# Head attention: one value job moved from step 15 to step 24, and the ring of score tiles counted through all batches

## The reference

```
x = x + L0_xattn(layernorm(x), ctx, ids, pointers)   # window of 3 context rows for each token
x = x + L0_ffn(layernorm(x))                         # 8 experts, top 2, and a shared one
x = x + L1_xattn(layernorm(x), ctx, ctx)             # 16 heads of width 8 over 1601 context rows
x = x + L1_ffn(layernorm(x))                         # 8 heads, 16 experts, top 2
```

```
qh, kh, vh = split_heads(q @ Wq + bq), split_heads(k @ Wk + bk), split_heads(v @ Wv + bv)
scores = einsum('bhsd,bhtd->bhst', qh, kh) / sqrt(8)
out = softmax(scores) @ vh ;  return merge_heads(out) @ Wo + bo
```

## Time and profile before

| what | us |
| --- | --- |
| median of 3 runs (1922.25 to 1926.83) | 1922.9 |
| time of the profiled execution | 1942.84 |
| its span, first to last instruction | 1940.5 |
| head attention, first to last exponential | 671 to 1491 |
| PE busy / DVE busy / ACT busy / POOL busy | 1731.0 / 1040.0 / 1349.4 / 241.4 |
| granted clock of TensorE, mean | 0.979 |

### The profile page before, as it was taken

One profiled execution on the slowest core, in us unless ns is written; L12 is line 12 of the kernel. 1 busy time (PEld: TensorE's weight loads), 2 busy tenths in 40 slices (PEclk: granted clock), 3 DMA queues, 4 the chain that ended last, 5 costly groups with the idle time before them and its releaser, 6 DMA issues.

```text
span 1940.5 us, 47109 instructions
## 1 busy us (share of the span) xinstructions
PE 1731.0 (89%) x19832; PEld 1118.3 (58%) x19832; DVE 1040.0 (54%) x2670; ACT 1349.4 (70%) x1589; POOL 241.4 (12%) x160
## 2 busy tenths in 40 slices
PE   0546999999999989999999999999988899999998
PEld 0335999999998844444444455445444455555554
DVE  3996222222224355555555555555456877777773
ACT  0334444444443489999999999999998667766765
POOL 6346000000000110000000000000000212111222
PEclk9777999999999999999999999999999999999999
DMA  8001000000000233333333333333250000000000
GB/s 284 1 1 47 1 1 1 1 1 1 1 1 1 63 81 84 81 83 82 81 80 81 76 80 71 80 75 79 62 128 4 1 6 6 7 1 6 6 6 11
DMA packets 36213, 85.68 MB, mean 44 GB/s; under 512 B 10649, under 2 KB 23330, under 8 KB 35618
## 3 DMA queue, kind: packets, MB, share of 16 engines
q1 hardware_dynamic: 33954, 76.30, 16.6%
q0 software_dynamic: 2048, 6.36, 1.1%
HBM read 30.43 MB, written 2.10 MB: 17 GB/s over the span
## 4 chain that ended last, share of the span: by engine, by line
PE 50%; ACT 20%; issue 12%; DVE 9%; DVEq 1%; ACTq 0%; POOL 0%; POOLq 0%
ACT C_probs L1909 18%; PE C_ps_s L692 14%; PE C_ps_s L679 10%; PE C_ps_s L1149 6%; PE C_ps_s L1158 6%; DVE C_den_t L2073 3%; PE C_ps_o L1806 3%; PE C_ps_o L1174 2%; PE C_ps_s L1791 2%; PE C_ps_p L1139 2%; DVEq L2036 1%; DVE D_gated L1377 1%; PE C_ps_p L1740 1%; PE C_ps_s L697 1%; PE C_ps_p L1747 1%
## 5 line engine op out<-in xcount | busy, mean ns | idle before, releaser
L1909 ACT ACTIVATE C_probs<-C_ps_s 128x1024 f32<-128x1024 f32 x832 | 774.0, 1062 | 47.4 <-PE C_ps_s L1791 47.0
L1806 PE MATMUL C_ps_o<-C_probs,C_values 128*16 128x256 f32 x6656 | 440.1, 382 | 6.4 <-DVE C_o_t L2069 5.7
L1237 ACT ACTIVATE D_hidden<-C_ps_s,D_b_up 128x1024 f32<-128x1024 f32 x256 | 275.4, 1114 | 135.6 <-PE C_ps_s L1149 135.3
L753 ACT ACTIVATE B_hidden<-C_ps_s,B_b_up 128x512 f32<-128x512 f32 x288 | 192.0, 689 | 197.0 <-PE C_ps_s L679 196.4
L692 PE MATMUL C_ps_s<-B_w_down,B_hidden 128*128 128x128 f32 x2304 | 277.5, 277 | 0.0
L692 PEld LDWEIGHTS C_ps_s<-B_w_down,B_hidden 128*128 128x128 f32 x2304 | 271.4, 193 | 10.4 <-ACT B_hidden L753 1.2
L1791 PE MATMUL C_ps_s<-C_queries,C_keys 32*128 32x256 f32 x3328 | 211.3, 328 | 39.0 <-ACT C_probs L1909 37.7
L1806 PEld LDWEIGHTS C_ps_o<-C_probs,C_values 128*16 128x16 f32 x6656 | 154.3, 95 | 145.0 <-ACT C_probs L1909 8.6
L1791 PEld LDWEIGHTS C_ps_s<-C_queries,C_keys 32*128 32x128 f32 x3328 | 126.6, 183 | 168.2 <-ACT C_probs L1909 121.5
L856 DVE SCALAR_TENSOR_TENSOR B_acc<-C_ps_s,B_gate,B_acc 128x128 f32<-128x128 f32 x224 | 63.1, 344 | 273.5 <-PE C_ps_s L692 273.5
L1149 PE MATMUL C_ps_s<-D_up_in,D_w_up_r 128*128 128x512 f32 x512 | 186.6, 446 | 1.8 <-ACT D_hidden L1237 1.8
(11 more groups left out here) (275 smaller groups left out, 1951.4 us busy)
## 6 DMA issues: line engine op xcount, KB each, us to landing
C_keys<-C_k_hi SPq DMA_DIRECT2D x128, 200.1 KB, 4.2
C_ctx_t<-ctx_t_dram SPq DMA_DIRECT2D x16, 800.5 KB, 4.4
C_keys<-C_k_lo SPq DMA_DIRECT2D x64, 200.1 KB, 4.1
C_queries<-C_q_hi SPq DMA_DIRECT2D x128, 32.0 KB, 2.3
B_w_up<-L_ffn_w_up_dram SPq DMA_DIRECT2D x1, 2304.0 KB
B_w_down<-L_ffn_w_down_dram SPq DMA_DIRECT2D x1, 2304.0 KB
C_queries<-C_q_lo SPq DMA_DIRECT2D x64, 32.0 KB, 2.3
C_queries<-C_blank SPq DMA_DIRECT2D x16, 128.0 KB, 2.6
```

The lines of the kernel that those rows point to most:

```text
L753: nc.scalar.activation(hidden[:, e % HB, c, :], ps_h[c][:], ACT.Gelu, bias=b_up[:, u:u + 1]).then_inc(s_hid, 1)
L1237: nc.scalar.activation(hidden[:, u % RING, :, :], ps_u[u % 2][:], ACT.Gelu, bias=b_up[:, u % PAIRS:u % PAIRS + 1]).then_inc(s_hid, 1)
L1806: m = T.matmul(ps_o[32 * j:32 * j + 2 * DK, g % 2, :], values[:, parity, kt, g * HG + j, :], probs[:, slot(parity, 2 * step + j // 2), j % ...
L1909: nc.scalar.activation(probs[:, slot(parity, n)], ps_s[bank(parity, n)][:], ACT.Exp, scale=SCORE_SCALE1).then_inc(s_exp, 1)
```

## The change

The value job with index 13 moves from step 15 to step 20, and the four value jobs that stood at steps 20 to 23 stand at steps 21 to 24. `FIN_AFTER`, the number of jobs that piece 0 of `finish` waits for, is counted from `JOB_AT` and goes from 14 to 13. Since no job stands at step 15 any more, PE waits for the branch's `s_top_read` ahead of piece 0 at step 16 as well. The score tile of a unit is now counted over all units of all batches, and `scores` always waits for the unit three places before, in step 0 too.

```diff
-        JOB_AT = {u: n for n, u in enumerate((*range(8), 9, 10, 11, 12, 13, 15, *range(20, 24)))}
+        JOB_AT = {u: n for n, u in enumerate((*range(8), 9, 10, 11, 12, 13, *range(20, 25)))}
...
-        def bank(parity, n):
-            return (n + parity * (UNITS % SRING)) % SRING
-
-        def bank_before(parity, n):
-            at = n - 1
-            while (bank(parity, at) if at >= 0 else bank(1 - parity, UNITS + at)) != bank(parity, n):
-                at -= 1
-            return at
+        def bank(k, n):
+            return (UNITS * k + n) % SRING
...
-                    before = max(bank_before(parity, 2 * step + i) for i in range(2))
-                    wait(pe, s_exp, UNITS * k + before + 1)
+                    wait(pe, s_exp, UNITS * k + 2 * step + 2 - SRING)
...
-                            m = T.matmul(ps_s[bank(parity, 2 * step + j // 2)][:, j % 2, i, :],
+                            m = T.matmul(ps_s[bank(k, 2 * step + j // 2)][:, j % 2, i, :],
...
                             if last:
                                 pe.wait_ge(experts.s_job_done, experts.before_choice)
+                            elif n == min(FIN_AT):
+                                pe.wait_ge(s_top_read, TOP_READS * (k + 2) + 1)
                             finish(k - 1, 1 - parity, jobs_to(k + 1) + (0 if last else FIN_AFTER), FIN_AT[n])
```

More of the change, by code:

```diff
@@ L1634, in head_attention @@
         done = ForExperts(
-            home=home, ps_p=ps_p, ps_o=ps_o, ps_u=[ps_s[bank(1, UNITS - 3)], ps_s[bank(1, UNITS - 2)]],
-            ps_e=ps_s[bank(1, UNITS - 1)], s_exp=s_exp, exps=UNITS * BATCH, s_fin_read=s_fin_read, fins=BATCH)
+            home=home, ps_p=ps_p, ps_o=ps_o, ps_u=[ps_s[bank(BATCH - 1, UNITS - 3)], ps_s[bank(BATCH - 1, UNITS - 2)]],
+            ps_e=ps_s[bank(BATCH - 1, UNITS - 1)], s_exp=s_exp, exps=UNITS * BATCH, s_fin_read=s_fin_read, fins=BATCH)
         experts = head_experts(ctx, nc, io, x_sb, ident, norm_after, done)
@@ L1908, in exps @@
                             act.wait_ge(dense.s_down, dense.downs - 2 + n // 2)
-                        nc.scalar.activation(probs[:, slot(parity, n)], ps_s[bank(parity, n)][:], ACT.Exp,
+                        nc.scalar.activation(probs[:, slot(parity, n)], ps_s[bank(k, n)][:], ACT.Exp,
                                              scale=SCORE_SCALE1).then_inc(s_exp, 1)
```

## The result

The kernel after takes 1905.04 us (median, 1900.41 to 1907.5), the kernel before on the same chip 1922.58; the ratio is 0.9893 [0.9878, 0.9908]. The prediction said 1905.7. The medians are 17.5 apart; the ratio stands for 20.6 less, its interval for 17.7 to 23.5. So an agreement to a few tenths of a microsecond is in part luck.

A forecast was written before the change was run, and what follows sets the result against it. ACT's back-to-back exponentials were taken to pace head attention, so only the pauses between them cost time. 11.3 - 0.5 + 0.9 + 5.5 = 17.2 us off the median 1922.9 gave 1905.7; own range 1902 to 1909, full range 1899 to 1914.

The forecast's parts named there:

- Part 1: Job leaves step 15, batches 1 to 13: pauses at units 32 and 34 go, smaller one at 36; gain 11.3 us.
- 13 x 1.2: Sign in the table of waits: PE's piece 1 of finish waits for POOL's multiply, some 13 x 1.2 us in all.
- Part 2: A job arrives at step 24: costs nothing in ordinary batches, covered by step 25; batches 0 and 14 differ.
- Batch 0: Pause ahead of unit 32 goes whole, but step 23's fuller job waits 0.24 more for DVE: +0.9 us.
- Batch 14: Statistics on DVE delay emptying step 23's job, so unit 50 comes 1.4 late, against a 0.87 gain: -0.5 us.
- Part 3: Seven odd-to-even batch borders: scores(0) waits for unit 50 only, the 0.68 pause and 0.10 overlap go; gain 5.5 us.
- (a): POOL's multiply lets PE go later than its span ends, gain at unit 36 vanishes: 4.5 us left, 1918.4; chance 0.08.
- (b): Batch borders gain nothing because scores(0) of even batches waits for a landing: gain 11.7, 1911.2 us; chance 0.06.
- (c): All idle time at units 32 and 34 goes, without piece 1 waiting for POOL: gain 32.2, 1890.7 us; chance 0.03.
- (d): Placing chain ends later than step 0 in 15 batches; slower once a further 1.1 us late each; chance 0.03.

The follow-up runs named there:

- the run with the job alone: Kernel before with its own choice of score tiles, but value jobs moved to the new steps and the new wait ahead of piece 0: 1910.38 us, ratio 0.9933.
- the run with the ring alone: Kernel after with the value jobs where they stood before, so score tiles are counted through all batches: 1919.07 us, 0.9977 of the kernel before.
- three products on POOL: Three unused 128 x 128 products ahead of POOL's second multiply half: 1939.84 us added to the kernel after, 1932.64 us added to the kernel before.
- one product: Kernel after with one unused 128 x 128 product ahead of the second half of POOL's multiply: 1912.59 us, ratio 0.9941.

## Why the prediction was right

**Part 1, 11.3.** Right in place and mechanism: scores(16) and (17) in time, piece 1 waits for POOL, unit 36 at 2.44 behind POOL's start. The size was a little low. The 13 pauses of batches 1 to 13 sum to 11.0, mean 0.85, with overlap 12.3; the same batches had 24.9 at units 32 and 34, so 12.6 went. The place of the excess of 1.3 is the branch. The last inversion of DVE in batch 3 of the kernel after, to be read beside the earlier trace rows:

```profile
839.95 1.75 DVE L2068 RECIPROCAL C_den_t<-C_den_t 128x256 f32<-128x256 f32 x1 [1.70 <-DVEq L2056]
```

DVE's idle time ahead of this inversion sums to 25.0 over batches 1 to 13 before and to 23.3 after, 1.65 less. It differs from execution to execution: over batches 1 to 14 it is 25.2 to 27.5 in the seven profiled executions of kernels without a job at step 15, and 27.4 to 29.4 in the three with one. So the excess may be chance; that the change shortens the branch a little isn't ruled out. And the pause ahead of unit 36 follows it batch by batch: it is this idle time less 0.93 to 0.96 in batches 1 to 13 (1.70 and 0.76 here). Because of the shorter branch the wait of PE for POOL came to 10.2 in all and not to 13 x 1.2, too; besides, the table of waits counts from the end of a record (1.06 for weigh) and the prediction from 0.87, which is 0.19 in each batch. The small pauses ahead of unit 30 in batches 6, 7 and 9 are missing as well (about 1.1 with overlap). I don't count that to the change: the run with the job alone (0.35 and 0.26) and the two runs with more work on POOL in the kernel after have such pauses in the same order of work on PE, so they differ between executions.

**Part 2.** Step 24 costs nothing in any batch, right. Batch 0: 1.07 and 0.59 became 0.82, with the overlap 0.9 as predicted. Batch 14: the pause ahead of unit 50 is there, 1.10 where 1.2 was expected, ended as described, by DVE's late emptying; PE waits 1.20 for it at 1397.11. The batch comes out at +0.1 instead of -0.5, since its pause ahead of unit 36 is only 0.87: DVE's idle time at the branch was 2.42 in this batch before and 1.89 after.

**Part 3, 5.5.** All seven pauses at the borders are gone, and no wait of step 0 names a transfer. The run with the ring alone gives 4.6, with 5.5 inside its interval.

**The sum.** 12.6 + 1.1 + 0.9 + 0.1 + 5.5 = 20.2 in the pair of profiled executions, less 1.2 at the start of batch 0 (pauses of 3.68 and 0.45 for 2.20 and 0.69, the clock at 0.79 from 662 to 670), is 19.0 against the 18.95 measured; predicted were 17.2, the medians say 17.5 and the ratio 20.6. Taking the saving of one execution off the median held because the 19.9 between them lay ahead of the stage.

**The rivals.** (a) falls: in all fourteen batches POOL is named as the releaser of piece 1, and in each of them PE starts 0.05 or 0.06 behind the end of its recorded span. The Trainium skill (Perfetto Trace Analysis, section GPSIMD Engine Instruction) calls that span unreliable; for this tensor_tensor the trace disagrees. (b) falls by the ring alone. (c), all idle time gone at 1890.7, needed piece 1 not to wait for POOL. With `finish` a step later it doesn't, and that kernel takes 1894.4; with the statistics moved as well, which (c) didn't count on, it is 1891. The price of the rival was about right and its condition was missing. (d), a late placing chain, shows nowhere, even in kernels another 14 us faster.

## What to carry to other kernels

Idle time of the bottleneck is worth what is left after the next-latest event has been put in its place: find that event by the same sum of start, duration and hand-over before counting the pause as gain, and what it takes is also what the next change can win. Where a fixed chain ends in the middle of a written-out order, look at moving its consumer one slot as well as the work around it: here that brought 7 to 11 us on top of the job's 13. And a wait added to an engine that is itself nearly saturated has to be priced with the chance that its clock falls afterwards.

## What was not expected of the hardware

**A short wait of PE can be followed by a stretch at the lower clock.** In the run with the ring alone, batch 13, PE idles 0.60 ahead of weigh and 1.24 behind the branch, and the next runs of matmuls take 1.6 to 1.7 times as long as usual (timeline of PE):

```profile
1345.28 1.08 PE L1741 MATMUL C_ps_p<-C_wv,C_ctx_t 128*32 128x128 f32 x16 [1.24 <-DVEq L2054]
1346.29 0.80 PE L1784 MATMUL C_ps_s<-C_queries,C_keys 32*128 32x256 f32 x8
1347.02 1.82 PE L1799 MATMUL C_ps_o<-C_probs,C_values 128*16 128x256 f32 x16
```

The granted clock from 1346 to 1350 is 0.67; over the two microseconds from 1345.48 it is 0.50, which is 1.2 of 2.4 GHz. With three products on POOL it was 0.50 in batch 6, then 0.65 and 1.00 again. The Trainium skill (TensorE: Matmul & The Clock Gate, Part 1) gives this gate two levels; the trace agrees, if 0.65 and 0.67 are means over stretches that hold both. The length of the wait alone doesn't decide. In the run with the ring alone the clock fell in batch 1 too, behind a wait of 0.72 (0.61 and 0.53 in the four microseconds from 744), and stayed at 1.00 behind 1.16 in batch 9. With three products it fell behind 2.14 and stayed behind 2.23 and 2.65, and with one product it stayed behind every wait, up to 1.72. What decides these runs don't show.

**The branch on a register takes a varying time.** DVE's idle time ahead of the inversion behind it was 1.43 to 2.42 from batch to batch in the execution before and 1.31 to 2.25 in the one after, with the same code ahead of it; the pause ahead of unit 32 was 0.69 to 1.83 before. (The 2.55 in batches 13 and 14 of the run with the ring alone hold a lower clock as well.) A saving that ends at such an instruction carries this spread with it.
